# Turning x of every odd tile by VectorE blocks and a round trip through DRAM, in place of TensorE transposes

## What is computed

```python
xc = x.reshape(Bsz, nc, L, H, P)
xdt = xc * dtc[..., None]
scores = jnp.einsum('bclhn,bcshn->bchls', Cc, Bc) * Lmat
Ydiag = jnp.einsum('bchls,bcshp->bclhp', scores, xdt)
states = jnp.einsum('bclhn,bchl,bclhp->bchpn', Bc, decay_states, xdt)
Yoff = jnp.einsum('bclhn,bchpn,bchl->bclhp', Cc, prev, jnp.exp(cs))
Y = (Ydiag + Yoff).reshape(Bsz, S, H, P) + x * D[None, None, :, None]
```

## Time and profile before

| | us |
|---|---|
| median of three runs | 1758.66 |
| the profiled execution, its own time | 1758.21 |
| span of its trace | 1756.4 |
| TensorE busy | 1742.4 (99%) |
| VectorE busy | 1402.7 (80%) |
| ScalarE busy | 1221.6 (70%) |
| GpSimd busy | 1232.1 (70%) |

### The profile page before, as it was taken

The page is one execution under the profiler, slowest core; times in us unless marked ns, Lnnn a source line. Parts: engine busy times, 40 slices in busy tenths (PEclk is TensorE's granted clock), DMA queues, the critical chain, the costliest instruction groups (busy, mean ns, idle before and its releaser), DMA issues.

```text
span 1756.4 us, 30305 instructions
## 1 busy us (share of the span) xinstructions
PE 1742.4 (99%) x10301; PEld 1459.3 (83%) x10301; DVE 1402.7 (80%) x2211; ACT 1221.6 (70%) x2456; POOL 1232.1 (70%) x877
## 2 busy tenths in 40 slices
PE   8999999999999999999999999999999999999999
PEld 6788888888888888888888888888888888888877
DVE  7978788878878788778788788878887887868941
ACT  6986677777776777777867778767877787643320
POOL 5677777777876787677776777677777787576630
PEclk9999999999999999999999999999999999999999
DMA  5442333333333343333333333333323343236522
GB/s 196 165 131 99 116 116 112 98 123 109 134 105 94 104 135 109 108 101 117 118 102 118 116 111 108 103 109 127 123 91 103 109 135 107 76 98 175 146 78 96
DMA packets 122595, 202.84 MB, mean 115 GB/s; under 512 B 23056, under 2 KB 60560, under 8 KB 122192
## 3 DMA queue, kind: packets, MB, share of 16 engines
q1 hardware_dynamic: 120720, 197.32, 34.8%
q10 hardware_dynamic: 1728, 3.65, 0.5%
HBM read 193.57 MB, written 7.34 MB: 114 GB/s over the span
## 4 chain that ended last, share of the span: by engine, by line
PE 94%; DVE 3%; issue 1%; POOL 1%; DMA 0%; ACT 0%; SPq 0%; DVEq 0%; ACTq 0%; POOLq 0%
PE bank L143 17%; PE bank L145 16%; PE bank L144 16%; PE bank L573 10%; PE bank L609 7%; PE bank L677 7%; PE bank L679 7%; PE bank L678 6%; PE bank L888 3%; PE bank L738 3%; DVE z L1246 1%; PE bank L700 0%; DVE lm L1267 0%; PE bank L720 0%; DVE acc L1337 0%
## 5 line engine op out<-in xcount | busy, mean ns | idle before, releaser
L964 ACT ACTIVATE lm<-lm,hp 128x128 f32<-128x128 f32 x1024 | 313.1, 389 | 0.8
L1246 DVE SCALAR_TENSOR_TENSOR z<-bank,cw_all,z 128x511 f32<-128x511 f32 (+2 forms) x384 | 286.9, 747 | 13.3 <-ACT z L1000 4.2
L1611 POOL TENSOR_TENSOR conv_lo<-raw_x,conv_hi 128x512 fp32r<-128x512 f32 x124 | 203.7, 1643 | 129.4 <-ACT conv_hi L901 129.3
L143 PE MATMUL bank<-xn_hi,conv_hi 128*128 128x512 f32 x640 | 261.4, 408 | 1.9 <-DVE z L1246 1.4
L1306 DVE TENSOR_TENSOR xdt<-bank,hp 128x512 f32<-128x512 f32 x128 | 88.2, 689 | 212.4 <-PE bank L738 212.4
L145 PE MATMUL bank<-xn_hi,conv_lo 128*128 128x512 f32 x640 | 250.6, 392 | 0.0
L144 PE MATMUL bank<-xn_lo,conv_hi 128*128 128x512 f32 x640 | 249.5, 390 | 0.0
L1594 POOL TENSOR_TENSOR yt<-yt,ec 128x384 f32<-128x384 f32 x128 | 146.8, 1147 | 139.3 <-DVE ec L1315 107.9
L1280 DVE SCALAR_TENSOR_TENSOR lm<-lm,gm 128x1024 f32<-128x1024 f32 x128 | 225.3, 1760 | 7.8 <-ACT lm L964 7.2
L1578 POOL TENSOR_TENSOR y_lo<-yt,y_hi 128x512 fp32r<-128x512 f32 x128 | 180.1, 1407 | 52.4 <-ACT y_hi L1035 52.4
L143 PE MATMUL bank<-xn_hi,gate_hi 128*128 128x512 f32 x512 | 212.9, 416 | 0.0
(11 more groups left out here) (152 smaller groups left out, 4051.5 us busy)
## 6 DMA issues: line engine op xcount, KB each, us to landing
lm<-cs_d SPq DMA_DIRECT2D x128, 512.0 KB, 4.5
raw_x<-w_conv_dram SPq DMA_DIRECT2D x128, 256.0 KB, 3.5
ec<-e_d SPq DMA_DIRECT2D x256, 96.0 KB, 2.7
raw_o<-w_out_dram SPq DMA_DIRECT2D x64, 256.0 KB, 3.0
raw_g<-w_gate_dram SPq DMA_DIRECT2D x61, 256.0 KB, 3.2
raw_g<-w_conv_dram SPq DMA_DIRECT2D x16, 256.0 KB, 3.2
raw_o<-w_conv_dram SPq DMA_DIRECT2D x14, 256.0 KB, 3.4
q_raw<-w1q_dram SPq DMA_DIRECT2D x10, 256.0 KB, 3.9
```

Source lines behind the costliest of these rows:

```text
L143: pe.matmul(dst, a_hi, b_hi, start=(i == 0), stop=False)
L964: e = act.activation(lm[m % LM_BUFS][:, u, :], lm[m % LM_BUFS][:, u, :], ACT.Exp, bias=hp[bd.seq][:, Q_CS, k1, u:u + 1])
L1246: dve.scalar_tensor_tensor(dst[:, d:SEQ], src[:, 0:SEQ - d], cw_all[:, bd.group, pos, 3 - d:4 - d], dst[:, d:SEQ], ALU.mult, ALU.add).then ...
L1611: pool.tensor_tensor(conv_lo[kx % 2][:, :, :], raw_x[:, kx % 2, :].rearrange("p (k j) -> p k j", k=KT), conv_hi[kx % 2][:, :, :].bitcast(F ...
```

## The change

For the tiles t that are odd, from 7 to 123 (`by_blocks`; 59 of them, four in each full body: k = 1, 3, 5, 7), `turn_x` is left out on TensorE. Instead:

- In step t-2, after `ec`, VectorE transposes `xt` of tile t in 32x32 blocks into `z[:, 1, :]`, the half of z that no convolution uses then.
- SyncE writes that half to a DRAM buffer `xb_d` (256 KB), and after that reads it back with four DMAs of 32 partitions each, in runs of 32 elements (128 bytes), into `xdt[1]`. The write is placed ahead of `load_rows`, the four reads behind the `ec` loads and ahead of `raw_o`, `raw_g` and B and C.
- In step t, VectorE makes `xw` from `xdt[1]` first and then scales `xdt[1]` in place. Both operands of both products now lie in SBUF; before, x lay in the bank.
- `two_diags` in these steps waits for `st_done` in place of `xw_done` (the bank is no longer filled by `turn_x`), and ScalarE's copy into `z[:, 1, :]` of tile t+2 waits for the write `xb_out`.

```diff
+def by_blocks(t):
+    return paired(t) and t % 2 == 1 and t >= TILES - 1
...
+            def blocks_out(t):
+                if by_blocks(t):
+                    sp.wait_ge(blk_done, blocks_before(t) + 1)
+                    wait(sp, xtok_in, 16 * BLK * blocks_before(t))
+                    sp.dma_start(xb_d.rearrange("g i c b j -> (g i) (c b j)"), z[:, 1, :]).then_inc(xb_out, 16)
+
+            def tokens_in(t):
+                if by_blocks(t):
+                    sp.wait_ge(xb_out, 16 * (blocks_before(t) + 1))
+                    sp.wait_ge(yd_done, t - 1)
+                    for b in range(BLK):
+                        sp.dma_start(xdt[1][32 * b:32 * b + 32, :].rearrange("i (c g j) -> i c g j", c=NC, g=BLK),
+                                     xb_d[:, :, :, b].rearrange("g i c j -> i c g j")).then_inc(xtok_in, 16)
...
+                blocks_out(n + 2)
                 load_rows(body, k)
...
+                tokens_in(n + 2)
                 bd, k1 = at(body, k, 1)
                 for group, pos in out_piece(bd, k1):
...
-                pe.wait_ge(xw_done, n + 1)
+                if by_blocks(n):
+                    pe.wait_ge(st_done, n)
+                else:
+                    pe.wait_ge(xw_done, n + 1)
                 diag(n, ps_x)
...
-                if bd.exists():
+                if bd.exists() and not by_blocks(n + 1):
                     pe.wait_ge(xs_done, TILES * bd.n + k1 + 1)
...
+                    if by_blocks(m - 2):
+                        act.wait_ge(xb_out, 16 * (blocks_before(m - 2) + 1))
                     act.activation(z[:, kx % 2, :], ps_a[:, :], ACT.Identity, scale=cw_all[:, bd.group, pos, 3:4],
...
+                    if by_blocks(n):
+                        dve.wait_ge(xtok_in, 16 * BLK * (blocks_before(n) + 1))
+                        dve.wait_ge(st_mm, n)
+                        dve.tensor_tensor(by_head(xw[:, :]), by_head(xdt[1][:, 0:(NC - 1) * P]),
+                                          per_token(hp[body.seq], Q_DEC, k, NC - 1), ALU.mult).then_inc(xw_done, 1)
+                        dve.wait_ge(xw_done, n + 1)
+                        dve.tensor_tensor(by_head(xdt[1][:, :]), by_head(xdt[1][:, :]),
+                                          per_token(hp[body.seq], Q_DT, k, NC), ALU.mult).then_inc(xdt_done, 1)
+                    else:
...
+                if by_blocks(n + 2):
+                    dve.wait_ge(xs_done, n + 3)
+                    dve.transpose(z[:, 1, :], xt[:, (k + 2) % 4, :]).then_inc(blk_done, 1)
```

More of the change, by code:

```diff
@@ L49 @@
 LM_BUFS = 4
+BLK = P // 32
 SH = 4
@@ L111, in paired, with blocks_before @@
     return TILES // 2 <= n < TILES * (BODIES - 1) + TILES // 2
+def by_blocks(t):
+    return paired(t) and t % 2 == 1 and t >= TILES - 1
+def blocks_before(t):
+    return sum(1 for u in range(t) if by_blocks(u))
 def group_exists(group):
@@ L166, in build @@
     hp_d = nc.dram_tensor("hp_d", (SEQS, P, NQ, GROUPS, TILES, 2 * NC), F32).ap()
+    xb_d = nc.dram_tensor("xb_d", (BLK, 32, NC, BLK, 32), F32).ap()
     mamba_d = nc.dram_tensor("mamba_d", (TT, P, DIM), F32).ap()
@@ L316, in build @@
         tx_done = sem("tx_done")
+        blk_done, xb_out, xtok_in = sem("blk_done"), sem("xb_out"), sem("xtok_in")
         xdt_done, xw_done = sem("xdt_done"), sem("xw_done")
@@ L432, in load_rows @@
                                  .partition_broadcast(P)).then_inc(row_in[m % LM_BUFS], 16)
+            def blocks_out(t):
[10 more added lines that the diff above has]
+                                     xb_d[:, :, :, b].rearrange("g i c j -> i c g j")).then_inc(xtok_in, 16)
             def step(body, k):
+                n = TILES * body.n + k
                 bx, kx = at(body, k, 5)
@@ L1300, in step @@
                 if body.exists():
[L1302 to L1310, removed]
+                    if by_blocks(n):
[7 more added lines that the diff above has]
+                    else:
+                        dve.wait_ge(tx_done, n + 1 - blocks_before(n))
+                        if k == 0:
+                            wait_hp(dve, body)
+                        wait(dve, yd_done, n - 1)
+                        dve.tensor_tensor(by_head(xdt[n % 2][:, :]), by_head(ps_x[:, :]),
+                                          per_token(hp[body.seq], Q_DT, k, NC), ALU.mult).then_inc(xdt_done, 1)
+                        wait(dve, st_mm, n)
+                        dve.tensor_tensor(by_head(xw[:, :]), by_head(ps_x[:, 0:(NC - 1) * P]),
+                                          per_token(hp[body.seq], Q_DEC, k, NC - 1), ALU.mult).then_inc(xw_done, 1)
                 if pv.exists():
```

## The result

The changed kernel takes 1831.62 us (median of 4 runs, 1826.48 to 1832.73), the kernel before 1758.68: a ratio of 1.0409, 95% interval 1.0388 to 1.043. The transposes that are gone are 25 us, so about 98 us were added. By the pages 77 of them are TensorE standing: its idle time is 1830.9 - 1740.1 = 90.8 us, and was 14.0 before.

What follows compares the result with a forecast made beforehand. TensorE's own work, 94% of the chain, was taken to bound the kernel, VectorE nearly level in k = 1 and 3. -25.4 + 13 + 15 + 8 = +10.6 on 1758.2 gave 1769 us with the median's 0.45; range 1736 to 1800.

Steps and rivals of the forecast that it cites:

- Removed: On TensorE, the four transposes of each of 59 odd tiles go, 0.43 us a tile: 25.4 us saved.
- The block transpose: On VectorE in odd steps, 0.6 us each (0.3 to 1.2); 0.55 lost in k = 1 of even bodies.
- Two operands in SBUF: xw and xdt of odd steps wait out GpSimd operations: 1.3 us in k = 1 of even bodies, 15 in k = 3.
- The queue: On SyncE, reads delay raw_o by 4.4 us; ScalarE stands 2.9 in even steps, 0.13 a pair comes through: 8 us.
- a sign of being wrong: In SyncE's queue, raw_o still landing in about 3 us would show the forecast wrong.
- the queue decides: Rival: small packets near 88 ns make raw_o 6 to 8 us late, 0.8 a pair reaches TensorE: 1808 us, chance 0.12.
- Every product waits: Rival: xw and xdt each meet a GpSimd operation, always in k = 3: 1777 us, 1785 with the queue; chance 0.12.
- Covered: Rival: VectorE's waits for GpSimd fall elsewhere and the reads are short: 1740 us, at best 1733; chance 0.32.

Runs made afterwards that it cites:

- late reads: The four reads moved behind raw_o, raw_g and the raw tile of B and C in SyncE's queue, against the changed kernel: 1780.46 us.
- bank operands: xw and xdt of odd tiles read the bank ps_x instead of xdt[1], against the changed kernel, x of these tiles left out: 1801.26 us.

## Why the prediction was wrong, step by step

- **Removed, 25.4 us:** the price of a turn was right (10.93 to 10.50, 10.03 to 9.58). The premise "if everything else stays covered" failed in k = 0: 15 of the 59 turns covered a wait for GpSimd's sum of squares: 10.46 to 10.42 in k = 0, about 6 us of the 25 not gained.
- **The block transpose, 0.6:** it is 0.70, within the bounds. The estimate of 1.24 from the Trainium skill's figure (VectorE: DVE Perf Modes, The three transpose paths) did not hold for this form. I had it cost 4 us; alone it costs 9 to 12. In k = 1 of even bodies it costs 0.70 a step where I had 0.55; and k = 3 of even bodies, in which I had given it no part, grew by 0.72 (15.32 to 16.05).
- **Two operands in SBUF, 9 + 15 = 24 us** (4 of the 13 us for k = 1 are the transpose): right in mechanism and size, 23 to 30 by three pairs of runs. The place was right in the main. With late reads the bank operands take 1.84 us off k = 1 of even bodies and 1.72 off k = 3 of odd ones, but only 0.25 off k = 3 of even ones (1.67 with early reads). The wait at the end of k = 1 that I had put before the turn is not there; TensorE stands a little earlier, for `yt`. The trace agrees with the rule of the Trainium skill (SBUF — State Buffer, Who interferes with whom) in the two products followed above: 1.66 and 1.65 instead of 0.55 and 0.69.
- **The queue, 8 us: this is the step that failed.** The size of the delay was foreseen: I said that the four reads take 2.2 us to issue (2.64 in the case above), and that ScalarE stands about 2.9 us in an even step (3.34 at the longest, 126 / 59 = 2.1 on average). Its cause was not: I had `raw_o` wait 4.4 us for the transfer of the small packets, and it landed in 2.9 us (median of all), which I had named as a sign of being wrong. It was issued later; it did not travel longer. What I then took was that 0.13 us a pair reaches TensorE, because ScalarE has 7 us of slack in two steps; it was 51 / 59 = 0.87 (47 / 59 = 0.79 with the bank operands). The slack was an average over the two steps, and lies in the odd step: of the 190 us in which ScalarE waits for the gate's bank (L1020 <- L156), all but 2 fall in steps with odd k. In the even step the late ScalarE copies the gate out of its bank late, which TensorE's next product needs, and squares y late. TensorE's waits for these two, L753, L603 and L154 in the list, are at k = 0, 4 and 6, most of them in even bodies. I followed only one way from ScalarE to TensorE, by the exponentials, and that one has room: VectorE stood 3.0 us in all for them in the changed kernel.
- **The rivals:** "the queue decides" is what happened, and my price for it, 1808, with 0.12, was low as well; even at its full 2.9 us a pair I had capped it at 0.8. "Every product waits" (1777) is near to the late reads' 1780.5. "Covered" (1740) was not reached even without turns, early reads and transpose: 1745.65.

The sum as measured: 1831.6 less 51 (queue), 26 (turns), 9 (transpose) is 1745.6; 12 are left to 1733, of which about 6 are k = 0 and some 3 are k = 3 of even bodies (15.32 against 14.85). The rest was not followed up. By what single way the delay reaches k = 3 (1.46 and 0.97 us less with late reads) wasn't separated from the turns there, which the delay also moves.

## What to carry to other kernels

A DMA that nobody waits for soon can still be the dearest instruction of a change, by what stands behind it in its issuing queue: place it behind the loads that are due first. Slack is a property of a step and a path, so follow a delayed engine through every product that it hands on, not just through the largest. And an instruction that is taken off the bounding engine gives its time only if nothing right behind it was waiting under its cover.

## What was not expected of the hardware

Four DMAs of 512 runs of 128 bytes (64 KB each) landed 2.6 us after issue (median), sooner than the loads of 256 KB. The `raw_o` loads that stand right behind them were not held up by them: 0.62 us to issue and 3.34 to land, against 0.58 and 3.38 for the same loads in the kernel before. What the small runs change is their own issue, 0.64 us in place of 0.42, and that four times in front of what is due. So the time to landing shows nothing of this queue's trouble; the time at which a load is issued and its reader's wait do.
